# An attention and mixture-of-experts block: expert weights on chip, stack loads in four pieces, two norms by way of memory, routing by chunks

## The reference, cut to what matters

```python
x = L0_attn_x                                  # (1, 2048, 128)
h = _layernorm(x) * (1 + ca) + sa              # sa, ca, ga, sb, cb, gb: from silu(c) @ wmod
x = x + ga * attention(h)                      # 16 heads of 8, causal, a linear bias with a slope per head
h = _layernorm(x) * (1 + cb) + sb
logits = h @ router_w.T                        # 8 experts
top_w, top_idx = top_k(softmax(logits), 2); top_w = softmax(top_w)
y_e = silu(h @ w1[e].T) @ w2[e].T              # 128 -> 512 -> 128, fp32, one expert e
x = x + gb * sum over a token's two experts of top_w * expert_scale[e] * y_e
```

## Time and profile before

| | us |
|---|---|
| median of 3 runs (603.47 to 609.74) | 604.99 |
| the profiled execution: its time | 603.54 |
| its span in the trace | 601.7 |
| PE busy | 505.1 (84%) |
| DVE busy | 457.1 (76%) |
| ACT busy | 403.2 (67%) |
| POOL busy | 168.3 (28%) |

### The profile page before, as it was taken

The page is one execution under the profiler, slowest core; times in us unless marked ns, Lnnn a source line. Parts: engine busy times, 40 slices in busy tenths (PEclk is TensorE's granted clock), DMA queues, the critical chain, the costliest instruction groups (busy, mean ns, idle before and its releaser), DMA issues.

```text
span 601.7 us, 15390 instructions
## 1 busy us (share of the span) xinstructions
PE 505.1 (84%) x5876; PEld 267.1 (44%) x5876; DVE 457.1 (76%) x756; ACT 403.2 (67%) x776; POOL 168.3 (28%) x286
## 2 busy tenths in 40 slices
PE   4756787889989999997999998988888979999870
PEld 2422232333343343241343242334435978888760
DVE  3789899989989989986998988984758546553442
ACT  4922556669888888876888887777787455444430
POOL 3310000000040122210312100304074852850884
PEclk9965899999999999998999999989999999999995
DMA  6692600000064300351100000100014656776742
GB/s 152 206 278 61 107 2 2 1 4 3 12 106 166 102 3 3 141 89 36 20 2 4 2 2 8 21 2 4 1 49 124 201 155 176 222 218 187 210 135 74
DMA packets 44024, 49.48 MB, mean 82 GB/s; under 512 B 7160, under 2 KB 33976, under 8 KB 43320
## 3 DMA queue, kind: packets, MB, share of 16 engines
q1 hardware_dynamic: 41568, 43.88, 27.0%
q0 software_dynamic: 2048, 4.20, 2.4%
q10 hardware_dynamic: 336, 0.42, 0.2%
HBM read 31.70 MB, written 16.58 MB: 80 GB/s over the span
## 4 chain that ended last, share of the span: by engine, by line
PE 37%; POOL 9%; ACT 6%; issue 6%; DVE 5%; DMA 4%; SPq 2%; POOLq 0%; DVEq 0%; ACTq 0%
PE pv L708 14%; PE b L741 10%; ACT probs L1245 5%; PE b L680 5%; POOL raw L1410 3%; POOL pause L1382 3%; DVE part L968 3%; POOL slot_scratch L1389 2%; PE b L655 2%; DMA xt<-slot_scratch 2%; PE b L815 2%; PE b L825 2%; ACT raw L1217 1%; DMA sums_scratch<-raw 1%; PE b L610 1%
## 5 line engine op out<-in xcount | busy, mean ns | idle before, releaser
L1245 ACT ACTIVATE probs<-b 128x512 f32<-128x512 f32 (+1 forms) x576 | 298.6, 571 | 89.1 <-PE b L655 35.4
L968 DVE TENSOR_REDUCE part<-b 128x2 f32<-128x1024 f32 (+2 forms) x320 | 327.1, 1061 | 31.2 <-PE b L680 15.9
L708 PE MATMUL pv<-probs,v_cur 128*32 128x256 f32 (+1 forms) x2432 | 177.8, 373 | 3.4 <-issue 3.0
L680 PE MATMUL b<-aug 52*128 52x512 bf16 (+3 forms) x640 | 117.8, 368 | 22.3 <-DVE part L968 19.8
L741 PE MATMUL b<-aug 55*128 55x512 bf16 (+3 forms) x640 | 114.9, 357 | 24.8 <-ACT probs L1245 20.2
L741 PEld LDWEIGHTS b<-aug 55*128 55x128 bf16 x640 | 36.8, 93 | 137.8 <-ACT probs L1245 128.1
L708 PEld LDWEIGHTS pv<-probs,v_cur 128*32 128x32 f32 x2432 | 50.2, 109 | 71.8 <-issue 45.4
L825 PE MATMUL b<-aug,hst 128*128 128x128 f32 x424 | 57.0, 278 | 1.1 <-DVE aug L1097 1.0
L815 PE MATMUL b<-hTt,aug 128*128 128x128 f32 x424 | 57.0, 278 | 0.5 <-ACT hTt L1266 0.5
L825 PEld LDWEIGHTS b<-aug,hst 128*128 128x128 f32 x424 | 52.4, 195 | 1.6 <-DVE aug L1097 0.9
L815 PEld LDWEIGHTS b<-hTt,aug 128*128 128x128 f32 x424 | 52.2, 194 | 0.7 <-issue 0.7
(11 more groups left out here) (150 smaller groups left out, 370.2 us busy)
## 6 DMA issues: line engine op xcount, KB each, us to landing
aug<-in_w1T SPq DMA_DIRECT2D x53, 256.0 KB
xt<-slot_scratch SPq DMA_DIRECT2D x53, 64.0 KB
y_scratch<-aug SPq DMA_DIRECT2D x53, 64.0 KB
slot_scratch<-slots SPq DMA_DIRECT2D x3, 1024.0 KB, 7.3
aug<-q_scratch SPq DMA_DIRECT2D x6, 384.0 KB
aug<-k_scratch SPq DMA_DIRECT2D x6, 384.0 KB
w2T_sb<-in_w2T SPq DMA_DIRECT2D x1, 2048.0 KB, 7.6
q_scratch<-pieces SPq DMA_DIRECT2D x4, 384.0 KB, 2.8
```

Source lines behind the costliest of these rows:

```text
L680: ins = mm(pair[half][:, at_:at_ + w], q_aug[buf][n, b, t:t + P], k_aug[buf][n, b, c * CW:c * CW + w], start=True, stop=True)
L708: return mm(pv[32 * hh:32 * hh + 32, c0:c1], v_cur[:, kb, hh, :], probs[:, step_ % 2, hh, at_:at_ + c1 - c0], start=(kb == 0 and c0 == 0), ...
L968: ins = nc.vector.tensor_reduce(dst, b1[:, slot:slot + 2, at_:at_ + w], AX.X, ALU.max)
L1245: nc.scalar.activation(probs[:, p % 2, hh, 0:w], b2[:, (n2 - 1) % RING2, 0:w], ACT.Exp).then_inc(exp_done, 1)
```

## The change

1. **Expert weights.** The whole of w1T (2 MB) is loaded in eight pieces of 256 KB during steps 21 to 28 of group 3 into the buffer that aug0 leaves free. DVE's stage(j) now copies the expert's w1 slice (128x512) to one of 4 buffers, and w2 is no longer copied: PE loads the expert's number into a register itself (owner_of) and down reads w2T at that register. SP's load_tile keeps only the DMA of the tokens. The experts start on place_s of 1 rather than 2.
2. **Stack loads.** The four DMAs of a stack go out at four steps (STACK_AT), the second to the fourth behind a wait on exp_done; the bias rows follow the fourth.
3. **Norms.** Chunks 0 and 1 of group 3 go by way of memory like the other groups, with 128x16 tiles (LAST_OUT to LAST_INVERSE), and POOL multiplies and adds (scale_last). The two scale_sums and add_sums on DVE at steps 5 to 15 go.
4. **Routing.** route works on one chunk (4 tiles) at a time, and its steps in the program of DVE and ACT are placed anew; PROJECT, TURN, LOGITS and COUNT move by a step or two.

```diff
-SCALED_AT, ADDED_AT = {5: 0, 12: 1}, {14: 0, 15: 1}
-PROJECT = {17: 0, 18: 1, 24: 2}
...
+STACK_AT = {True: [START[1], START[1] + 2, START[1] + 4, START[1] + 6], False: [0, 2, 4, 6]}
+LAST_OUT, LAST_IN, LAST_INVERT, LAST_BACK, LAST_INVERSE = [4, 11], [6, 13], [INVERT, 14], [9, 15], [11, 16]
+LAST_SCALE = {14: 0, 18: 1}
+PROJECT = {16: 0, 19: 1, 24: 2}
...
-                    if p == (START[1] if first else 0) and not last:
-                        take(sp, aug_free, 1)
-                        load_stack(sp, g + 1, (g + 1) % 2, 0, NC_, aug_in)
-                        if not first:
+                    if p in STACK_AT[first] and not last:
+                        piece = STACK_AT[first].index(p)
+                        if piece == 0:
+                            take(sp, aug_free, 1)
+                        else:
+                            sp.wait_ge(exp_done, HG * (NSTEP * g + p))
+                        load_stack(sp, g + 1, (g + 1) % 2, 0, NC_, aug_in, [piece])
+                        if piece == 3 and not first:
                             load_alibi(sp, g + 1, (g + 1) % 2, aug_in)
...
+                    if last and p in W1_AT:
+                        n0 = W1_AT.index(p) * E * F // len(W1_AT)
+                        n1 = n0 + E * F // len(W1_AT)
+                        sp.wait_ge(exp_done, HG * (NSTEP * g + p))
+                        sp.dma_start(w1T[:, n0:n1], a["w1T"][:, n0:n1]).then_inc(w1_in, 16)
...
-                e = sp.value_load(expert[0:1, j:j + 1], min_val=0, max_val=E - 1)
-                if j >= DEEP:
-                    sp.wait_ge(up_ps, j - DEEP + 1)
-                sp.dma_start(w1s[:, k, :], a["w1T"][:, ds(e * F, F)]).then_inc(w1s_in[k], 16)
...
-            def down(j):
-                k = j % DEEP
-                pe.wait_ge(w2s_s, j + 1)
+            def owner_of(j):
...
+                return pe.value_load(expert[0:1, j:j + 1], min_val=0, max_val=E - 1)
+
+            def down(j, e):
                 pe.wait_ge(silu_s, j + 1)
...
-                    last = mm(b1[:, 2 + j % 2, 0:C], hst[:, j % 2, f, :], w2s[:, k, f, :], start=(f == 0), stop=(f == FC - 1))
+                    last = mm(b1[:, 2 + j % 2, 0:C], hst[:, j % 2, f, :], w2T[:, ds(e * FC + f, 1), :], start=(f == 0), stop=(f == FC - 1))
...
                 if j:
-                    down(j - 1)
+                    down(j - 1, owner_)
+                owner_ = owner_of(j)
...
-                    dve.wait_ge(down_ps, j - DEEP + 1)
-                V.tensor_copy(w2s[:, j % DEEP, :, :], w2T[:, ds(e * FC, FC), :]).then_inc(w2s_s, 1)
+                    dve.wait_ge(up_ps, j - DEEP + 1)
+                V.tensor_copy(w1s[:, j % DEEP, :], w1T[:, ds(e * F, F)]).then_inc(w1s_s, 1)
...
+            def scale_last(q):
+
+                pool.wait_ge(last_inverse_in[q], 16 * HG)
+                pool.wait_ge(yT_s, NC_ * (G - 1) + q + 1)
+                y, scaled = unit_y(q), raw_y(G - 1, q)
+                own.inc(nc.gpsimd.tensor_tensor(scaled, scaled, last_inverse[:, q * CW:(q + 1) * CW], ALU.mult))
+                own.wait()
+                nc.gpsimd.tensor_tensor(y, y, scaled, ALU.add).then_inc(y3_s, 1)
```

More of the change, by code:

```diff
@@ L289, in build @@
         rl = sb("rl", [P, 4, CW // 32])
-        sums = sb("sums", [P, T // 32])
+        sums = sb("sums", [P, T // 32 + 2 * CW // 32])
+        last_inverse = sb("last_inverse", [P, 2 * CW])
         inverse = sb("inverse", [P, T])
@@ L381, in build, with load_stack @@
         block = ctx.enter_context(nc.Block())
-        def load_stack(e, g, buf, c0, c1, done):
+        def load_stack(e, g, buf, c0, c1, done, pieces_=range(4)):
             t0, t1 = c0 * CW, c1 * CW
-            for half in range(2):
+            for piece in pieces_:
+                half = piece // 2
                 rows_ = slice(HALF * half, HALF * half + ALIBI0)
-                for aug, dram in ((q_aug, q_dram), (k_aug, k_dram)):
+                for aug, dram in [((q_aug, q_dram), (k_aug, k_dram))[piece % 2]]:
                     src = dram.rearrange("(g b s d) p t -> g s (d p) b t", b=PAIRS, s=2, d=D)
@@ L416, in raw_y, with last_part @@
             return raw[:, g % 2, j * CW:(j + 1) * CW]
+        def last_part(q):
+            return sums[:, T // 32 + q * CW // 32:T // 32 + (q + 1) * CW // 32]
         def tile_outs(j):
@@ L497, in group @@
                             sp.dma_start(inverse[row:row + D, :], inverse_dram[h:h + 1, :].to_broadcast([D, T])).then_inc(inverse_in, 16)
+                    if last and p in LAST_INVERSE:
+                        q = LAST_INVERSE.index(p)
+                        sp.wait_ge(last_back_out, 16 * (q + 1))
+                        for h in range(HG):
+                            row = 32 * h + D * g
+                            sp.dma_start(last_inverse[row:row + D, q * CW:(q + 1) * CW], last_back[q, h:h + 1, :].to_broadcast([D, CW])).then_inc(last_inverse_in[q], 16)
                     for u in turns(p, first, last):
@@ L781, in step @@
                             turn_late(TURN[p])
-                        for c in LOGITS.get(p, []):
-                            logits(c)
+                        if p in LOGITS:
+                            logits(LOGITS[p])
                         if p in COUNT:
@@ L846, in _ @@
                     count(NPART - 1)
-            down(TILES - 1)
+            down(TILES - 1, owner_)
         @block.vector
@@ L951, in group @@
                         upto = min(upto, NTASK)
[L952 to L955, removed]
                     if g and p == INVERT:
                         dve.wait_ge(sums_in, 16 * g)
-                        nc.vector.reciprocal(sums[:, :], sums[:, :]).then_inc(invert_s, 1)
+                        nc.vector.reciprocal(sums[:, 0:T // 32], sums[:, 0:T // 32]).then_inc(invert_s, 1)
+                    if last and p in LAST_INVERT:
+                        q = LAST_INVERT.index(p)
+                        dve.wait_ge(last_in, 16 * (q + 1))
+                        nc.vector.reciprocal(last_part(q), last_part(q)).then_inc(last_s, 1)
                     while at < upto:
@@ L1126, in _ @@
             scale_tokens(2)
-            route(0, 5)
+            for k in range(1, 5):
+                route(1, k)
+            keep_logits(2)
+            route(2, 0)
             for j in range(DEEP - 1):
                 stage(j)
-            keep_logits(2)
-            for k in range(5):
-                route(1, k)
+            for k in range(1, 5):
+                route(2, k)
             place_part(1)
-            route(1, 5)
+            for c in range(3):
+                route(c, 5)
             scale_sums(NC_ - 1)
@@ L1148, in _ @@
                 if j in LATE_ROUTE:
-                    route(NPART - 1, LATE_ROUTE[j])
+                    route(NC_ - 1, LATE_ROUTE[j])
                 if j in LATE_PLACE:
@@ L1204, in route_exp @@
             def route_exp(k, b):
-                n = slice(*PARTS[k])
+                n = slice(TPC * k, TPC * (k + 1))
                 if b == 0:
@@ L1242, in group @@
                                 copy_values(*((g, START.index(p) - 1) if p else (g - 1, NC_ - 1)))
+                            if last and (p, hh) in ROUTE_EXP:
+                                route_exp(*ROUTE_EXP[p, hh])
                             n2 += 1
@@ L1250, in group @@
                         features(TURN[p], 1)
-                    if last and p in ROUTE_EXP:
-                        route_exp(*ROUTE_EXP[p])
+                    if last and (p, HG) in ROUTE_EXP:
+                        route_exp(*ROUTE_EXP[p, HG])
                 if last:
@@ L1436, in group @@
                             scale_values(g - 1, j)
+                    if last and p in LAST_SCALE:
+                        scale_last(LAST_SCALE[p])
                     for q in range(3):
```

73 lines of the change are left out of this document (48 added, 25 removed).

## The result

The changed kernel takes 599.95 us (median of 12 runs, 596.66 to 602.85) beside 607.72 us for the kernel before in the same comparison: a ratio of 0.9888, 95% interval 0.9855 to 0.992. It is faster by 1.1%, where 2.8% was forecast; 599.95 lies inside the range of 577 to 606. The ratio leaves slow runs out, while 607.72 is the median of all 12 runs of the kernel before, with one of 880.91 in a slow state. The profiled execution took 599.72 us, its span is 597.9 us against 601.7.

What follows compares the result with a forecast made beforehand. Loads, not matmuls, were taken to pace PE's experts' stage, with short attention stalls. First tile of part 1 at 487.0, 24 turns of 2.0 us, then 1.1 + 4.1 + 29.2 + 15.2 give 584.6, plus 1.84: 586.4 us; range 577 to 606.

Steps and rivals of the forecast that it cites:

- the 24 turns: Experts' stage, first tile of part 1 to down(37) on PE: 2.42 us a turn before, forecast 2.0.
- in all at 189.4, or 1 to 2 us more behind the piece's own 384 KB: Attention group 1: when the read of the sums lands, issued at 187.5 behind the fourth stack piece and bias rows.
- +4.4. Bounds: 0 ... and +8: Groups 1 and 2: DVE's reciprocal waits 2.2 us more in each for the sums, as stack loads are spread.
- the stall: PE idle 3.01 us at 275.81 in group 2, read as late instructions behind stack DMAs; spreading returns 4.5 us.
- put the loss on the sums: Sign of being wrong: groups 1 and 2 longer than before by more than 4.4 us together.
- the attention gains nothing: Rival: reads of the sums wait longer or the stall stays, everything 6 us later, 592.4 us; chance 0.10.
- The rule of the Trainium skill that was weighed: Instruction fetch is mostly hidden, so the stall isn't the fetch's, its 4.5 us stay; the sum becomes 590.9.
- P: PE's time per expert tile turn with weights on chip: taken as 2.0 us, ends 1.90 and 3.66.
- the rival of a slow sequencer: PE's register operations, 0.59 to 1.76 us a tile, become the experts' bound: 606 to 617 us; chance 0.17.
- norms and routing: Group 3's norms off DVE return 6 us, 3 per ACT stall; routing by chunks brings place of part 1 1 us earlier.
- the sum: Span by the gather of part 1: 487.0 + 24P + 1.1 + 4.1 + 29.2 + 15.2, giving 584.6 us.

Runs made afterwards that it cites:

- the burst: Changed kernel with all four stack pieces and the bias rows issued in one step again: 592.45 us, ratio 0.9804 to the kernel before.
- the pieces around the sums: Changed kernel with the third and fourth stack piece at steps 8 and 10 instead of 4 and 6: 586.71 us, ratio 0.9692.
- Three placements of the burst: Changed kernel with the stack's pieces in one go at step 0, behind the exps before step 1, or before step 2: 592.45, 594.12, 600.58 us.
- three loads in one run: Changed kernel with PE loading the expert's number three times per tile instead of once: 640.48 us, a single run.
- The later break: POOL does the last chunk's norm after 10 sends, not 8: 590.13 us with stack pieces at steps 0 to 3, 584.05 with the pieces around the sums.

## Why the prediction was right or wrong

The forecast span was 584.6 us, the measured one is 597.9. The 13.3 us are, from row to row: first tile of part 1 at 499.42 instead of 487.0, +12.4; the 24 turns +1.1; from there to the gather of part 1 -0.9; the gather of part 1 +0.6. The 12.4 are 10.9 of attention, less 1.75 of routing, plus 3.2 of sends.

**Wrong: what the spread loads cost.** The step that failed is "in all at 189.4, or 1 to 2 us more behind the piece's own 384 KB", and with it "+4.4. Bounds: 0 ... and +8". The issue was right to a tenth (187.5), the way from there was not: behind a 384 KB piece and four bias DMAs a 32 KB read took 6.1 us to land, and a DVE wait of 5.1 us cost PE and ACT a us more than itself, as the clock had fallen when they resumed. Whether the piece or the bias rows weigh more in the 6.1, no run separates. Group 1 lost 6.1 us, and group 2 some 7 (2.6 net of the stall). That is 13 instead of 4.4, outside the bounds, and the prediction's own sign of it came: groups 1 and 2 together 8.7 us longer than before, where more than 4.4 would "put the loss on the sums". The rival with the right mechanism, "the attention gains nothing", had a chance of 0.10; it has the attention end as before, and it ended 4.9 us later. Where the prediction put 1 to 2 us for the piece's bytes, the landing took 4.2 us more than before.

That two numbers of a table then give 586.71 us, beside the 586.4 forecast for the change, is luck. The forecast holds 4.4 for the sums, which that kernel doesn't pay; without them its span would be 580.2, and it is 586.2. The 6.0 us are 5.0 until the first tile of part 1 (487.60 instead of 482.6: mainly the sends, the norms and an attention that reaches group 1 a us later and takes 1.1 longer in it, less the routing) and 1.0 behind it.

**Right: the stall.** It vanished with the spreading and returned with the burst, 3.01 us both times. Its size was right too: group 2 takes 91.4 us with the pieces around the sums and 96.0 before, 4.6 us for the 4.5 forecast. Three placements of the burst tie the stall's length to the late instruction packet. The rule of the Trainium skill that was weighed (page "Runtime: NRT & Kernel Launch", section "Instruction fetch mechanics": mostly hidden) holds for a packet 1.9 us late here, and not for those 4.1 and 6.2 us late.

**Right: the weights.** P was 2.05 with the restart and 1.896 fed, against 2.0. The price of PE's register operations was near the lower bound (0.69 against 0.59 us); the rival of a slow sequencer was wrong in its price, and nearer than its chance of 0.17 said in its mechanism, since three loads in one run suggest that hardly any time was left.

**Right in sign, off in size: norms and routing.** 4.4 us instead of 6, as two stalls were 2.2 us each and not 3; 2.75 us of place instead of 1, just past the bound of 2.5.

**Missed: the sends.** That POOL would be late by 3.2 us wasn't in the sum, nor the clock behind the wait for tokens. The sends now start 1.9 us ahead of the experts, and POOL's break after eight of them depends on PE's progress; what comes earlier in one queue found its partner not yet there. The later break shows it: without the wait for the norm the stretch is 4.3 to 4.8 us shorter.

## What to carry to other kernels

A small transfer that an engine's queue waits for is worth more than the large one beside it: place the small one first and the large one where nothing small follows, and check the far end too, the first use of what was moved. When bulk loads are spread, look at what lies behind each new place in the same issuing queue, by landing time and not by issue time. A wait of a few us on PE costs its length and what the lower clock takes behind it (here 3.29 us of waiting brought 5 us at half the clock, 0.80 us none), so cutting one can give back more than itself.

## What the runs showed of the hardware

PE's semaphore operations take three times SP's, and its register operations don't: 301 ns for a load and 151 for the operation behind it, beside 268 and 152 on SP. PE's sequencer can be full while its array is not: 0.69 us of control work per 1.90 us turn are invisible, 0.94 more at one place of the turn cost 0.99. And a transfer burst of some 10 us can hold up an engine's own instructions: the packet inside it came 6.2 us late and PE stood for 3.01 us, 4.1 us late and it stood for 0.81, 1.9 us late and it didn't stand.
